# Graph attention on one core: scores as small matrix products of transposed K tiles instead of a spread Q and vector arithmetic

## The reference, cut to what matters

```
scores = jnp.einsum('ehd,ehd->eh', q[tgt], k[srcidx])
m = jax.ops.segment_max(scores, tgt, num_segments=n)
p = jnp.exp(scores - m[tgt])
s = jax.ops.segment_sum(p, tgt, num_segments=n)
w = p / (s[tgt] + 1e-16)
agg = jax.ops.segment_sum(w[:, :, None] * v[srcidx], tgt, num_segments=n)
```

## Time and profile before

| | |
|---|---|
| median of 3 runs | 3967.89 us (3965.73 to 3982.18) |
| the profiled execution | 3992.01 us |
| its span | 3990.3 us |
| PE busy | 3619.6 us, 91% |
| DVE busy | 2592.8 us, 65% |
| ACT busy | 852.3 us, 21% |
| POOL busy | 1154.0 us, 29% |
| mean granted clock of PE | 0.795 |

### The profile page before, as it was taken

One profiled execution on the slowest core, in us unless ns is written; L12 is line 12 of the kernel. 1 busy time (PEld: TensorE's weight loads), 2 busy tenths in 40 slices (PEclk: granted clock), 3 DMA queues, 4 the chain that ended last, 5 costly groups with the idle time before them and its releaser, 6 DMA issues.

```text
span 3990.3 us, 39943 instructions
## 1 busy us (share of the span) xinstructions
PE 3619.6 (91%) x12444; PEld 1449.9 (36%) x12444; DVE 2592.8 (65%) x5039; ACT 852.3 (21%) x3254; POOL 1154.0 (29%) x1109
## 2 busy tenths in 40 slices
PE   4998999999999998787979999999999969589899
PEld 3872333333333332345852222222222224244444
DVE  5113888887888887345127777777777733855655
ACT  3211232322333332011211111111111111022221
POOL 0002444443343432000024545545454500111200
PEclk7995999998999997898985555555555579789999
DMA  8224666665666664211245656565665621201100
GB/s 282 98 101 158 202 198 203 199 203 169 192 199 196 195 196 151 61 61 40 98 161 179 214 197 216 194 211 201 204 206 199 210 64 49 74 24 40 53 24 23
DMA packets 212672, 593.34 MB, mean 149 GB/s; under 512 B 32898, under 2 KB 39266, under 8 KB 212443
## 3 DMA queue, kind: packets, MB, share of 16 engines
q0 software_dynamic: 137088, 466.78, 36.3%
q1 hardware_dynamic: 75354, 123.80, 9.0%
HBM read 519.54 MB, written 96.68 MB: 154 GB/s over the span
## 4 chain that ended last, share of the span: by engine, by line
PE 46%; DVE 3%; issue 2%; ACT 1%; DMA 1%; POOL 0%; another core or an unknown queue 0%; SPq 0%; DVEq 0%; POOLq 0%; ACTq 0%
PE ps L838 15%; PE ps L871 9%; PE ps L1988 4%; PE ps L2009 4%; PE ps L1495 2%; PE ps L449 2%; PE ps L450 2%; PE ps L451 2%; PE ps L825 1%; PE ps L1433 1%; PE ps L1999 1%; PE ps L1779 1%; PE ps L1511 1%; DVE xT L1563 0%; PE ps L853 0%
## 5 line engine op out<-in xcount | busy, mean ns | idle before, releaser
L838 PE MATMUL ps<-G 32*128 32x512 f32 x1664 | 1129.8, 907 | 15.0 <-DMA G<-Qd,segE 13.9
L764 POOL DMA_INDIRECT Y<-KVd,srcE x654 | 660.0, 1009 | 1411.2 <-DMA KVd<-stage 712.4
L965 DVE TENSOR_REDUCE scores<-work 128x8 f32<-128x512 f32 x832 | 561.5, 675 | 0.9
L925 DVE TENSOR_TENSOR work<-Y,ps 128x512 f32<-128x512 f32 x654 | 443.6, 678 | 42.4 <-PE ps L838 28.9
L838 PEld LDWEIGHTS ps<-G 32*128 32x128 f32 x1664 | 282.3, 250 | 471.9 <-issue 334.3
L550 PE MATMUL ps<-WA,xT 128*128 128x512 f32 (+1 forms) x600 | 347.9, 663 | 7.8 <-DMA G<-in_MpT 7.8
L871 PE MATMUL ps<-G,onehot 128*32 128x512 f32 x832 | 315.7, 849 | 6.9 <-DVE G L933 3.5
L871 PE MATMUL ps<-stage,onehot 128*32 128x512 f32 x832 | 316.5, 851 | 0.0
L449 PE MATMUL ps<-Wh,xs 128*128 128x512 f32 (+1 forms) x600 | 236.1, 393 | 18.9 <-DVE xs L400 18.9
L2062 DVE SCALAR_TENSOR_TENSOR Y<-ps,WA,Y 128x512 f32<-128x512 f32 (+1 forms) x200 | 146.9, 748 | 152.5 <-PE ps L2009 143.2
L1013 ACT ACTIVATE stage<-ps,rec 128x64 f32<-128x64 f32 x832 | 182.0, 330 | 293.0 <-PE ps L871 293.0
(11 more groups left out here) (285 smaller groups left out, 4230.5 us busy)
## 6 DMA issues: line engine op xcount, KB each, us to landing
KVd<-stage SPq DMA_DIRECT2D x96, 256.0 KB, 2.0
aggd<-work SPq DMA_DIRECT2D x2, 7936.0 KB, 26.6
Qd<-stage SPq DMA_DIRECT2D x48, 256.0 KB, 2.0
G<-aggd SPq DMA_DIRECT2D x48, 256.0 KB, 3.5
Y<-KVd,srcE POOLq DMA_INDIRECT x654
Y<-in_x SPq DMA_DIRECT2D x4, 1536.0 KB, 14.1
mixd<-mt SPq DMA_DIRECT2D x24, 256.0 KB
stage<-in_x SPq DMA_DIRECT2D x24, 256.0 KB, 3.2
```

The source lines that it names most:

```text
L764: pool.indirect_dma_start(out=kvs[a], out_offset=None, in_=KVd[l][:, :], in_offset=bass.IndirectOffsetOnAxis(ap=srcE[:, i:i + 1], axis=0)) ...
L838: pe.matmul(QX[n % 3][:, :], hotT[j % 2][32 * q:32 * q + 32, P * x:P * (x + 1)], slotq[j % 3][32 * q:32 * q + 32, :], start=True, stop=Tru ...
L925: dve.tensor_tensor(work[:, n % 3, :], kvs[a][:, 0:D], QX[n % 3][:, :], ALU.mult).then_inc(qk, 1)
L965: dve.tensor_reduce(scores[:, b % 2, :].rearrange("p (h c) -> p h c", h=H)[:, :, r], h8(work[:, n % 3, :]), AXX, ALU.add).then_inc(sc, 1)
```

## The change

The scores are computed the other way round. Each K tile (128 edges by 512) is turned on PE in four 128x128 transposes (`turn_k`) into one of two PSUM banks, and ACT (three tiles of four) or DVE (one of four) copies it to SBUF (`empty_k`). The slots' Q rows are turned once a batch and laid out by head in `qblk`. The scores of a tile come out as 128 rows (8 heads by 16 slots) by 128 edges: a first product adds a large number where the edge does not belong to the slot (`maskA` against the turned one-hot matrix `hotT`), and four small products, each with 32 columns of output partitions, add minus Q times K. Four tiles make a group with one PSUM bank. Row minimum on DVE (`least`), exponential with its row sum on ACT (`exps_of`), one division on DVE (`normalise`); then the weights of the four tiles are turned back (`turn_p`), copied to `probs`, and used themselves as the stationary operand against V, head by head: 32 small products of 64 columns a group (`gather`). What DVE did over whole 128x512 tiles (L925, L965, L933) is gone, and so are the scans inside the loop.

The join's sequences are now 8 rows of 832 values; its four scans need no carries. What they need (the ends of each tile, row minimum and sum at tile borders) is gathered behind the loop, by one DMA (`ends_sp`), a few products (`stats_pe`) and vector operations. The mixer's steps are issued as before, four in a group of four tiles. The order in which the edge tiles are taken is now plain, 0 to 415.

```diff
+            def turn_k(n):
+                a = n % KVN[l]
+                bank = bank_of("k", n)
+                pe.wait_ge(kv_in[a], 16 * (kv_before(l, a) + n // KVN[l] + 1))
+                for k in range(4):
+                    mm = pe.transpose(bank[:, k * P:(k + 1) * P], kvs[a][:, k * P:(k + 1) * P], ident[:, :])
+                mm.then_inc(turned, 1)
...
+            def score(n):
+                g, i = divmod(n, 4)
+                j, c = divmod(n, NCH)
+                bank = SC[g % 2]
...
+                pe.matmul(bank[:, at], maskA[:, c, :], hotT[j % 3], start=True, stop=False, skip_group_check=True)
+                for k in range(4):
+                    mm = pe.matmul(bank[32 * k:32 * k + 32, at], qblk[j % 2][:, k, 2 * (c % 4) + c // 4, :],
+                                   kT[n % 3][:, k * P:(k + 1) * P], start=False, stop=True, skip_group_check=True)
+                mm.then_inc(sc, 1)
...
+            def gather(g):
+                x = g % 2
+                is_emptied(pe, l, PLACE["p", g])
...
+                for h in range(H):
+                    for i in range(4):
+                        a = (4 * g + i) % KVN[l]
+                        mm = pe.matmul(AG[32 * i:32 * i + 32, DH * h:DH * (h + 1)], probs[x][:, i, h, :],
+                                       kvs[a][:, D + DH * h:D + DH * (h + 1)], start=(x == 0 and h == 0), stop=(x == 1),
+                                       skip_group_check=True)
+                mm.then_inc(agg, 1)
...
+            for g in range(NQ + 2):
+                b, x = divmod(g, 2)
+                if g < NQ:
+                    turn_k(4 * g)
                 next(side, None)
+                if g < NQ:
+                    turn_k(4 * g + 1)
+                    score(4 * g)
+                if g >= 2:
+                    gather(g - 2)
+                next(side, None)
+                if g < NQ:
+                    turn_k(4 * g + 2)
+                    score(4 * g + 1)
+                next(side, None)
+                if g < NQ:
+                    turn_k(4 * g + 3)
+                    score(4 * g + 2)
+                    if x == 0 and b + 2 < NJ:
+                        turn_hot(b + 2)
+                    if x == 1 and b + 1 < NJ:
+                        turn_q(b + 1)
+                    score(4 * g + 3)
+                if 0 <= g - 1 < NQ:
+                    turn_p(g - 1)
+                next(side, None)
...
+            def exps_of(g):
+                act.wait_ge(mins, NQ * l + g + 1)
+                if g:
+                    is_turned(act, l, "p", g - 1)
+                for i in range(4):
+                    t = 4 * g + i
+                    last = act.activation(pT[:, P * i:P * (i + 1)], SC[g % 2][:, P * i:P * (i + 1)], ACT.Exp,
+                                          bias=smin[:, t:t + 1], scale=-1.0, accum_out=ssum[:, t:t + 1])
+                last.then_inc(exps, 1)
...
+            for g in range(NQ + 2):
+                b, x = divmod(g, 2)
+                if g < NQ:
+                    empty_k(4 * g)
+                if 0 <= g - 1 < NQ:
+                    exps_of(g - 1)
                 next(side, None)
+                next(side, None)
+                if g < NQ:
+                    empty_k(4 * g + 2)
+                next(side, None)
+                if g < NQ and 3 not in ON_DVE:
+                    empty_k(4 * g + 3)
+                if g < NQ and x == 1 and b + 1 < NJ:
+                    empty_q(b + 1)
+                next(side, None)
```

More of the change, by code:

```diff
@@ new lines, in build @@
+        smin = stage[:, 1, 0:ET]
+        pT = stage[:, 2, :]
+        qslot = stage[:, 3, :]
+        kT = [work[:, i, :] for i in range(3)]
+        hotT = [hotTs[:, i, :] for i in range(3)]
+        ends = mt[0:H, 512:512 + SEQ + 2].bitcast(I32).rearrange("p (t k) -> p t k", k=2)
+        snB = mt[:, 0:ET]
+        kv_in = [sem(f"kv_in{i}") for i in range(max(KVN))]
+        q_in, sct, seg_idx = sem("q_in"), sem("sct"), sem("seg_idx")
+        hot, turned, out_a, out_d = sem("hot"), sem("turned"), sem("out_a"), sem("out_d")
@@ L796, in attend_pool @@
+            at = KV
+            for g in range(NQ + 3):
+                b = g // 2
+                if g % 2 == 0 and b + 1 < NJ:
                     fetch_slots(b + 1)
-                if r == 4 and b >= 2:
+                while at < ET and (at - KV) // 4 <= g - 2:
+                    fetch(at)
+                    at += 1
+                if g % 2 == 0 and 0 <= b - 2 < NJ:
                     scatter(b - 2)
         def attend_pe(l, side):
-            E, J, G2 = ET * l, NJ * l, ET // 2 * l
@@ L969, in attend_act @@
-        def attend_act(l, side, begin):
-            E, J, G2, KV = ET * l, NJ * l, ET // 2 * l, KVN[l]
+            empty_hot(0)
+            empty_hot(1)
+            dve.memset(qslot, 0.0)
+            for i in range(2):
+                dve.memset(qblk[i], 0.0)
+                last = dve.memset(probs[i], 0.0)
+            last.then_inc(filled, 1)
+            for g in range(NQ + 2):
+                b, x = divmod(g, 2)
+                if g >= 2:
+                    empty_p(g - 2)
+                if 0 <= g - 1 < NQ:
+                    least(g - 1)
+                next(side, None)
+                if g < NQ:
+                    empty_k(4 * g + 1)
+                    if x == 0 and b + 2 < NJ:
+                        one_hot(b + 2)
+                next(side, None)
+                if 0 <= g - 1 < NQ:
+                    normalise(g - 1)
+                next(side, None)
+                if g >= 2 and x == 1:
+                    empty_agg(b - 1)
+                if g < NQ and 3 in ON_DVE:
+                    empty_k(4 * g + 3)
+                if g < NQ and x == 0 and b + 2 < NJ:
+                    empty_hot(b + 2)
+                next(side, None)
@@ new lines, in attend_act @@
+            empty_q(0)
+            for g in range(NQ + 2):
+                b, x = divmod(g, 2)
+                if g < NQ:
+                    empty_k(4 * g)
+                if 0 <= g - 1 < NQ:
+                    exps_of(g - 1)
+                next(side, None)
+                next(side, None)
+                if g < NQ:
+                    empty_k(4 * g + 2)
+                next(side, None)
+                if g < NQ and 3 not in ON_DVE:
+                    empty_k(4 * g + 3)
+                if g < NQ and x == 1 and b + 1 < NJ:
+                    empty_q(b + 1)
@@ L1312, in setup_pe @@
         def setup_pe():
-            pe.wait_ge(*next_of(jd_seen))
-            for d in range(2):
-                pe.transpose(PS[4 + d][0:1, 0:HC], smin[:, d:d + 1], ident[0:HC, 0:HC]).then_inc(*jp_made.up())
-            pe.wait_ge(*next_of(jd_seen))
             for b in range(TB):
```

846 lines of the change are left out of this document (380 added, 466 removed).

## The result

The changed kernel took 3888.15 us (median of 4 runs, 3881.57 to 3889.44) against 3969.9 us: ratio 0.977, 95% interval 0.974 to 0.980. It is faster by 2.3%, and outside the range 3290 to 3720. The forecast was 3390. Its profiled span is 3887.3 us.

What follows compares the result with a forecast made beforehand. PE was taken to bound both layer loops, at 2.4 GHz in layer 0 and 1.2 in layer 1. Span 3990 - 162 (layer 0) - 435 (layer 1) + 19 (join and rest) = 3412, median 3390 us; range 3290 to 3720.

Steps and rivals of the forecast that it cites:

- Layer 1: Second layer's loop: 1.68 us a tile from four close limits, 716 us instead of 1151, -435.
- Five hand-overs of 0.15 to 0.2: Waits between engines in layer 1's group chain, 0.15 to 0.2 us each, within 6.6 us a group, 1.65 a tile.
- Waits: Rival: in-order chain on PE, ACT and DVE 1 us a group longer than counted, +208, 3598 us; chance 13%.
- the transfers' limit of 1.64: Layer 1's DMA limit: 0.56 MB a tile at the burst's 343 GB/s, 1.64 us a tile.
- PE's limit of 1.46: PE's work in the new loop at 2.4 GHz: 11.7 us per eight tiles, 1.46 us a tile.
- changes of shape: PE switching into 32-column products and out again once a tile, 0.13 + 0.20 us, 2.6 us per eight tiles.
- rows 7: Profile rows at the kernel's start: three transposes fell from 0.88 to 0.52 us, read as clock rising on transposes alone.
- the rival of 1.2 GHz: Rival: clock stays at 1.2 GHz in layer 1, 2.69 us a tile, 1139 us instead of 716, 3813 us; chance 12%.
- Four quarters together: On PE, small products in four column quarters run at once: scores 0.21 us a tile, aggregation 1.0 a group.
- the rivals of 3706 and 4329: Rivals: small products two quarters at a time, 3706 us, 12%; or one after another, 4329 us, 5%.
- Mask product: PE's mask product in each tile's scores: one short pass of 0.06 us, 0.5 us per eight tiles.
- Layer 0: First layer's loop with the mixer: 2.65 us a tile, 1130 us instead of 1292, -162.

Runs made afterwards that it cites:

- e1: Changed kernel with layer 1 fetching only its first 17 K/V tiles and reusing those rows for all 416 tiles: 3440 us.
- e5: The changed kernel again, nothing altered, in a session with signals on time: 3549 us.
- e15: Changed kernel with five PSUM banks in layer 1, scatter ahead of the fetches and bf16 mask product, signals on time: 3412 us, ratio 0.8575 to the kernel before.
- e16: Changed kernel with layer 1 groups 28 to 51 fetched by plain transfers, 52 to 75 by index with 512 of 4096 bytes a row, signals late: 3848 us.
- e8: Changed kernel with layer 1 in seven stretches, one unchanged, the others varying fetches, passes, mask, transposes or scatter order, signals late: 3874 us.
- e6: Changed kernel with both operands of the mask product in bf16 instead of fp32r, signals on time: 3541 us.
- e7: Changed kernel without the mask product in layer 1, signals on time: 3549 us.
- sessions 1, 5 and 6: Groups of experiments on the changed kernel: layer 1 work removed (on time, 3440 to 3541 us); banks or all edits (late, 3856, 3855); fetch variants or all edits (on time, 3498, 3412).
- three experiments: Changed kernel with, in layer 1, no fetches after the first 17 tiles, one head aggregated, or no mask product: 3440, 3494 and 3541 us.

## Why the prediction was wrong

**Layer 1, the step that failed.** "Five hand-overs of 0.15 to 0.2" in the chain of a group, 6.6 us. PE's part of them took 2 to 3 us where signals were late, and a group 10.8 us in the profile on record: +404 us of the +475 on the span's 3412. No row of before could price this: in its layer 1 PE's signals stand at their passes' ends. My rival *Waits* had the kind right, a longer chain of waits, for other reasons (two banks, the fetch behind `gather`), and a fourth of the size in layer 1: 1 us a group for 3.9. It gave 3598.

**Where signals are on time** the same kernel took 3549 us, inside the range but not in the forecast's own 3290 to 3500, and layer 1 813 us for 716. That +97 goes with a wait I had not followed: the copy of the sums behind the scatter, on DVE ahead of the weights' copy, with two banks behind it. I had named POOL's queue and its price of 1.32 us, but not who waits for the landing of what stands last in it. With banks, scatter and mask changed the loop came to 678 us, 1.63 a tile, by the transfers' limit of 1.64. PE's limit of 1.46 was a little low: without fetches on time (e1) a tile took 1.68 with PE busy for 642 of 699 us, 1.54 a tile. Two of its terms were off and mostly cancel, the mask's (below) and the changes of shape: priced at 0.33 a tile, they are at most 0.15 of the 0.36 us that the score passes hold PE, and the four transposes behind them take 0.41 (2301.93 to 2302.34 in e5), no more than elsewhere.

**Clock.** 0.93 in layer 1 on time, 0.98 in e15, 1.00 in e16's stretch of plain transfers: it rises, as rows 7 said, and the rival of 1.2 GHz is gone. The granted clock reads 1.00 over the whole of rows 7's stretch, so only the passes' times show the rise there. On record it is 0.82, with PE idle for 28%, and alternates between the levels: 0.50 at 2508 to 2510 us, after PE had stood still for most of 2504 to 2506, and 1.00 at 2512 to 2514. In e8 the stretch with a quarter of the transposes had PE busy for 0.68 of the time like the stretch without the mask, but a clock of 0.69 against 0.81, which again speaks for transposes as work that holds the clock, though it is two stretches of one execution; the Trainium skill (TensorE: Matmul & The Clock Gate, PE-mode transpose) says that they do not count.

**Four quarters together.** Right. A tile's eight score passes take 0.36 us from their start to the next instruction's (2301.57 to 2301.93), forecast 0.21 and a change of 0.13. They start in two fours, 0.007 us apart in a four, and the last 0.15 us behind the first where I had asked for 0.12. The 64 aggregation passes took 1.0 us on time, as forecast (e6):

```profile
531.34 1.08 PE L912 MATMUL ps<-Y,G 128*32 128x64 f32 x64
532.35 1.13 PE L569 MATMUL ps<-WA,xT 128*128 128x512 f32 x2
```

One after another was tried in e8 for the aggregation: 13.5 for 11.1 us a group. So the rivals of 3706 and 4329 fell by their mechanism.

**Mask product.** Mis-sized: 0.06 forecast, 0.23 measured. It costs little, as e6 and e7 show.

**Layer 0.** 1130 forecast, 1153 on time, 1182 on record: 2.65 a tile became 2.70 on time. Late signals cost 29 us there instead of 307; I take it that PE had mixer products to do meanwhile, which no run shows by itself.

**Join and the rest.** +19 forecast, +38 measured (1585 against 1547 before).

**What stays open:** what differs between the sessions. It is not the chip's number alone (sessions 1, 5 and 6 ran on chips of one number), and for the changed kernel not the program. And by which way indexed fetches hold PE's signals but not those of ACT and DVE, whose recorded increments from 2498 to 2508 us stand within 0.02 us of their ends (some have no record).

## What to carry to other kernels

A kernel that was bound by PE's work and becomes bound by a ring of hand-overs feels delays that its old profile does not show: give each hand-over a spare buffer before you count on the sum of durations (three more banks gave 123 us here). In a queue that is issued in order, put first what somebody waits for soonest, here the scatter ahead of prefetches that have two groups of slack (what it gave by itself on time is not measured). And run the unchanged kernel in every session: three experiments here looked like three cures and were only another session.

## What the runs showed of the hardware

Signals of PE can come 2 to 3 us after its passes' modelled ends, then in a burst 0.06 us apart, while POOL issues indexed fetches, mostly with the last ones 1.1 us after POOL's series ends; plain transfers at 341 GB/s did not do it, and an eighth of the bytes by index at 37 GB/s did. Whether it happens changed between sessions, with 3549 or 3888 to 3979 us for one program. Passes of four different quarters of 32 output columns start 0.007 us apart, and 64 of them, of 64 columns each, took 1.0 us. An fp32r product of 128 columns held PE for 0.23 us and a bf16 one for 0.15.
